# The P V products of a pair of heads in one run of eight matmuls instead of two runs of four

## The reference

```
# block 1: 16 heads of 32, softmax over all 512 keys
q, k, v = split(xn @ W_qkv)                       # xn: normalised, scaled and shifted x
logits = einsum('bhqd,bhkd->bhqk', rms(q), rms(k)) * 32 ** -0.5
o = einsum('bhqk,bhkd->bhqd', softmax(logits), v)
y = o + o @ W_out
# block 2: 16 heads of 32, rotary parts, causal mask
scores = where(causal, einsum('bqhd,bkhd->bhqk', q, k) * 32 ** -0.5, min)
out = einsum('bhqk,bkhd->bqhd', softmax(scores), v) @ o_w
# then h + shared expert + 2 of 7 routed experts, chosen by a router
```

## Time and profile before

| | |
|---|---|
| median of 3 runs | 1286.12 us (1280.24 to 1286.89) |
| the profiled execution | 1280.03 us, of which the span 1278.3 us |
| attention stream | about 74 to 950 us of the span |
| experts | about 950 us to the end |
| granted clock of TensorE, mean | 0.955 |

### The profile page before, as it was taken

The page is one execution under the profiler, slowest core; times in us unless marked ns, Lnnn a source line. Parts: engine busy times, 40 slices in busy tenths (PEclk is TensorE's granted clock), DMA queues, the critical chain, the costliest instruction groups (busy, mean ns, idle before and its releaser), DMA issues.

```text
span 1278.3 us, 18202 instructions
## 1 busy us (share of the span) xinstructions
PE 1146.9 (90%) x5687; PEld 803.5 (63%) x5687; DVE 729.0 (57%) x1714; ACT 571.8 (45%) x1248; POOL 331.9 (26%) x275
## 2 busy tenths in 40 slices
PE   5989999999999799999979979988889999999970
PEld 5745555665566356557657657755657888888860
DVE  6565685477545756656545675475445774444433
ACT  3324464455444455555455554454454753222220
POOL 1313133201310131002012201200134464555530
PEclk9979999999999899999989999998979999999995
DMA  7054344235323732464476365385456745656669
GB/s 257 34 182 117 94 142 140 61 118 189 112 63 98 229 111 65 157 175 117 155 201 193 114 221 153 97 255 171 114 199 227 253 140 107 111 107 114 113 127 345
DMA packets 107470, 191.11 MB, mean 150 GB/s; under 512 B 26000, under 2 KB 36656, under 8 KB 105840
## 3 DMA queue, kind: packets, MB, share of 16 engines
q1 hardware_dynamic: 98560, 169.62, 42.6%
q0 software_dynamic: 8512, 19.93, 8.7%
q10 hardware_dynamic: 304, 0.40, 0.1%
HBM read 118.98 MB, written 65.53 MB: 144 GB/s over the span
## 4 chain that ended last, share of the span: by engine, by line
PE 73%; DVE 8%; DMA 7%; issue 4%; ACT 4%; SPq 3%; POOL 0%; DVEq 0%; ACTq 0%; POOLq 0%
PE psum L930 12%; PE psum L747 9%; PE psum L748 8%; PE psum L749 8%; PE psum L893 6%; PE psum L914 6%; PE psum L1008 4%; PE psum L1010 4%; PE psum L1009 4%; PE psum L756 3%; PE psum L1035 2%; PE psum L977 2%; PE psum L1037 2%; PE psum L1036 2%; DMA inverse_s<-prob_sums 1%
## 5 line engine op out<-in xcount | busy, mean ns | idle before, releaser
L1252 ACT ACTIVATE probs<-psum 128x512 f32<-128x512 f32 (+3 forms) x512 | 255.9, 517 | 224.9 <-PE psum L917 112.1
L1676 DVE TENSOR_REDUCE nmax<-psum 128x1 f32<-128x512 f32 x256 | 171.0, 685 | 112.7 <-PE psum L893 108.0
L893 PE MATMUL psum<-stack 96*128 96x512 f32 (+3 forms) x512 | 211.3, 418 | 17.9 <-DVE nmax L1679 11.0
L914 PE MATMUL psum<-stack 97*128 97x512 f32 (+3 forms) x512 | 202.3, 396 | 22.9 <-ACT probs L1252 20.5
L930 PE MATMUL psum<-probs,vals 128*33 128x512 f32 (+3 forms) x1024 | 212.2, 537 | 0.0
L893 PEld LDWEIGHTS psum<-stack 96*128 96x128 f32 x512 | 101.9, 199 | 80.7 <-issue 56.8
L1679 DVE CUSTOM_DVE_ANT_0 psum<-psum,causal 128x128 f32<-128x128 f32 (+3 forms) x256 | 122.7, 503 | 32.7 <-PE psum L893 31.5
L914 PEld LDWEIGHTS psum<-stack 97*128 97x128 f32 x512 | 101.7, 199 | 51.0 <-ACT probs L1252 27.2
L930 PEld LDWEIGHTS psum<-probs,vals 128*33 128x33 f32 x1024 | 50.3, 113 | 101.7 <-issue 69.5
L747 PE MATMUL psum<-w_hi,xh 128*128 128x512 f32 (+1 forms) x256 | 95.4, 373 | 3.2 <-DVEq L1532 1.6
L748 PE MATMUL psum<-w_hi,xl 128*128 128x512 f32 (+1 forms) x256 | 93.6, 366 | 0.0
(11 more groups left out here) (245 smaller groups left out, 2291.5 us busy)
## 6 DMA issues: line engine op xcount, KB each, us to landing
stack<-split_s SPq DMA_DIRECT2D x378, 128.0 KB, 3.2
split_s<-split SPq DMA_DIRECT2D x64, 512.0 KB, 3.0
inverse_sums<-inverse_s SPq DMA_DIRECT2D x124, 64.0 KB, 2.4
xt<-in_x_dram SPq DMA_DIRECT2D x4, 1024.0 KB, 5.4
x_s<-yt SPq DMA_DIRECT2D x4, 1024.0 KB, 5.5
xt<-x_s SPq DMA_DIRECT2D x4, 1024.0 KB, 5.0
yt<-in_x_dram SPq DMA_DIRECT2D x4, 1024.0 KB, 5.6
res<-x_s SPq DMA_DIRECT2D x4, 1024.0 KB, 8.4
```

The source lines that it names most:

```text
L893: sq.filled(nc.tensor.matmul(psum[:, sq.bank(M), 0:n], st[:, 0, t * P:(t + 1) * P], st[:, 1, 0:n], start=True, stop=True), M)
L914: last = nc.tensor.matmul(psum[:, bank, lo:S], st[:, 1, t * P:(t + 1) * P], st[:, 0, lo:S], start=True, stop=not masked)
L1252: sk.cleared(nc.scalar.activation(probs[:, M % NX, lo:S], psum[:, sk.bank(M), lo:S], ACT.Exp, scale=SCALE), M)
L1676: sq.cleared(V.tensor_reduce(out, psum[:, sq.bank(M), :], AX.X, ALU.max, negate=True), M)
```

## The change

Two constants are changed; the buffers of exponentials stay eight.

```
-GROUP = 4
-NX = 2 * GROUP
+GROUP = 8
+NX = 8
```

## The result

The change makes the kernel slower. Before 1285.38 us (1280.24 to 1286.89), after 1305.44 us (1303.82 to 1307.73), ratio 1.0184 with a 95% interval of 1.0155 to 1.0213. The forecast was 1282, the range 1270 to 1295: wrong in sign and outside the range.

What follows compares the result with a forecast made beforehand. TensorE, busy for 90% of the span, was taken to bound 35 of 64 pairs; -11.9 - 0.6 + 2.4 + 2.2 + 2.0 + 0 + 1.7 = -4.2 us, from 1286.12 to 1281.9 us; range 1270 to 1295.

Steps and rivals of the forecast that it cites:

- kind 1: 35 pairs in which TensorE is full: one run fewer saves 0.34 us in each, -11.9 us in all.
- the saving isn't a run's: Rival: the 0.34 us belongs to the change of data, not to entering a run; 1293.8 us, chance 0.05.
- Kind 6: The other 13 pairs: a chain beginning before the run sets their end, eight pv beside it as before; 0 us.
- Kind 2: Six light pairs paced by ACT, among pairs 5 and 6 of batches 0 to 3: gain eaten, -0.1 each, -0.6 us.
- Kind 3: Pairs 7 of batches 0 to 3, with transposes of x: waits for exponentials queued on ACT, +0.6 each, +2.4 us.
- kind 5: Pairs 4 and 5 of batch 0, full of DVE work: late copy and lost shelter, +1 each, +2.0 us.
- Kind 4: Four pairs where the maxima's DMA, taken to land in 1.8 us, delays the next pair's scores_t: +2.2 us.
- second rival: Late maxima after an unbroken half pair, at scores_t of step 8 in light pairs; 1294.4 us, chance 0.2.
- kind 7: One more fall of TensorE's clock, at places where it already has gaps: +1.7 us, from 0 to +7.
- Both still lie inside the run: Pairs 4 to 7: ACT's keys copy at step 0, 1.3 us late, and one DVE operation end within the run of eight.
- the prediction's example: A run of four at the lower clock, 3.59 us instead of 1.91, after scores_t had waited 1.9 us.

Runs made afterwards that it cites:

- by2: Kernel before with runs of two pv in place of four in all pairs, the same eight buffers; 1298.53 us, ratio 1.0139.
- packed2: Changed kernel with block 2's exponentials packed so that those of tile 0 wait for no product; 1307.75 us, ratio 1.0197.
- nine: Changed kernel with nine buffers of exponentials in place of eight in batches 0 to 2; 1307.33 us, ratio 1.02.
- wait: Kernel before, runs of four kept, with the exponentials of steps 0 and 1 waiting for pv as in the changed kernel; 1305.45 us, ratio 1.0168.
- fives: Kernel before with a run of eight only in pair 5 of batches 1 to 7; 1295.7 us, ratio 1.0095.

## Why the prediction was wrong, step by step

- **A run costs 0.34 us (kind 1): right as a price, too much as a gain.** A run of eight and its distance to the next product, the answer to the earlier trace rows:

```profile
227.77 0.40 PE L914 MATMUL psum<-stack 97*128 97x512 f32 x1
228.10 3.63 PE L930 MATMUL psum<-probs,vals 128*33 128x512 f32 x16
231.66 0.50 PE L893 MATMUL psum<-stack 96*128 96x512 f32 x1
```

  3.56 us to the next product, as forecast. 32 of the 35 pairs gained 9.4 us; without pair 2 of batch 0 and its shifted 1.8, 31 gained 7.5, 0.24 each and not 0.34: 0.35 in pairs 0 to 2 of batches 1 and 2, 0.02 to 0.13 in their other full pairs, 0.23 in batches 4 to 6. Their products are shorter there, which I hadn't priced apart; why the gain is smaller wasn't traced. The sorting failed in three (pair 3 of batches 0 and 1, pair 2 of batch 7), +6.7. The rival that the saving isn't a run's falls, by `by2` as well (0.33 a run).
- **Kind 6, "so 0": the step that failed.** I argued that the chain which sets these pairs' ends begins before the run, so that eight pv stand beside it before as after. In pair 5 of batch 6 that isn't so. Before, then after, from the half pair on:

```profile
834.62 1.70 PE L930 MATMUL psum<-probs,vals 128*33 128x512 f32 x8
...
840.02 0.30 PE L893 MATMUL psum<-stack 96*128 96x128 f32 x1 [2.63 <-DVE nmax L1679]
...
841.46 1.23 PE L930 MATMUL psum<-probs,vals 128*33 128x256 f32 x8
```

```profile
855.19 0.44 PE L893 MATMUL psum<-stack 96*128 96x128 f32 x1 [2.64 <-DVE nmax L1679]
...
857.81 3.33 PE L930 MATMUL psum<-probs,vals 128*33 128x512 f32 x16
```

  DVE's chain for that `scores` (a copy of transposed queries, the norms, the division, maxima) runs without a pause from the copy of step 2 on, before and after:

```profile
833.85 0.69 DVE L1517 TENSOR_TENSOR split<-psum,split 128x512 fp32r<-128x512 f32 x1 [1.11 <-ACT split L1094]
```

```profile
849.05 0.69 DVE L1517 TENSOR_TENSOR split<-psum,split 128x512 fp32r<-128x512 f32 x1 [1.12 <-ACT split L1094]
```

  That is over 2 us behind the end of the run of step 1 (831.66 and 846.61), not before its start, and `scores` follows 6.2 and 6.1 us later. The run of 1.7 us lay inside these 6 and cost nothing; after, the wait is still 2.64 us, and the pv come behind it, partly at the lower clock (3.33 us). `packed2` shows that the chain hangs on the run's end. There ACT doesn't wait for the buffer, and DVE's copy of step 0 stands 1.8 us before the end of the run of eight (848.62, the end 850.38) instead of at it (846.59, 846.61). Yet copy and `scores` keep their distance to the run's end (both line numbers are 16 higher in that kernel):

```profile
852.54 0.69 DVE L1533 TENSOR_TENSOR split<-psum,split 128x512 fp32r<-128x512 f32 x1 [1.25 <-ACT split L1110]
...
858.68 0.45 PE L909 MATMUL psum<-stack 96*128 96x128 f32 x1 [2.64 <-DVE nmax L1695]
```

  From the run's end to that `scores` it is 8.4 us before, 8.6 after and 8.3 in `packed2`: what sets the pair's end begins with the first products behind the run. Forecast 0 for 13 pairs, measured +14.8 (13.1 without the shift in pair 1 of batch 0), of which the pairs 5 of batches 5 to 7 hold 8.7. I had read such a chain in one pair only, pair 1 of batch 7, and that one came out 0.9 shorter.
- **Kind 2: right for pair 6, wrong for pair 5.** I walked through one pair, pair 6 of batch 3, and took it for six. It came out at 9.71 (forecast 9.5). In its neighbour, DVE, not ACT, sets the pace once the run is gone: +1.2 instead of -0.1, and +3.2, with a fall of the clock, in pair 5 of batch 2. DVE's 6.47 us of work in 9.70 had looked harmless, but 4.3 of them are one piece. The Trainium skill ("Perfetto Trace Analysis", Matmul Optimizations) wants matmuls back to back in batches, because the engine scales its power with its utilization. Larger batches went with less time in the full pairs (16.25 to 15.89 us) and with more in this one (9.70 to 10.89), at a granted clock of 1.00 in all four stretches, so neither difference bears on the page's reason.
- **Kind 3: mis-sized; kind 5: right in one pair of two.** Kind 3 took +5.8 against +2.4, of which pair 7 of batch 1 alone +2.4 with a fall of the clock (its clock is 1.00 in `nine`, and there it loses 0.87). The waits for exponentials did grow in pairs 7 of batches 0 to 2, by 0.5, 0.5 and 0.8 us; in batch 3 the new wait is another, 1.3 us of the transposes for DVE's copy of x. In kind 5, pair 5 of batch 0 lost 1.0 us, as forecast; pair 4 gained 2.9, because a wait of 2.3 us and a fall that stood in it are gone from it while pair 3 lost 4.5.
- **Kind 4, the maxima: near by luck.** +3.0 against +2.2, but `scores_t` waits for the maxima 2.2 us in three places, against 1.8 in two before. The only new wait of the four pairs, 1.0 us, is in pair 0 of batch 7, where the clock fell as well (+2.6); pair 5 of batch 4 lost 1.9 without any wait for maxima, and pair 6 of batch 2 got 1.8 shorter. In pair 6 of batch 3 the DMA left at 555.81 and its rows were used at 557.74, so it landed within 1.9 us, where I had taken 1.8. The second rival gave 1294.4, nearest to the result, but the runs with the maxima a step earlier rule late maxima out as the cause.
- **The clock (kind 7): mis-sized.** I took one more fall, +1.7. By the mean clocks, 141 us against 115 lie at the lower level, 26 more; the mean is within the 0.01 that I had allowed, so that test was too coarse. 26 us at half speed cost up to 13 if TensorE worked throughout. Pair 3 of batch 0 after shows one, the answer to the earlier trace rows:

```profile
149.76 0.67 PE L893 MATMUL psum<-stack 96*128 96x512 f32 x1 [1.47 <-DVE nmax L1676]
...
152.01 5.93 PE L930 MATMUL psum<-probs,vals 128*33 128x512 f32 x16
```

  After a wait of 1.47 us the products last 0.67 instead of 0.40 us, and the run of eight takes 5.93 instead of 3.63, 2.3 more; a run of four so caught took 1.7 more.
- **"Both still lie inside the run": right.** `nine` and `packed2` bear it out for batches 0 to 2 and block 2, the trace of pair 5 for batch 3.

What stays open: how much of the loss in the other 32 pairs is the clock's share, up to about half; why two pv after step 7 save half of it; whether the buffer's wait matters in batch 3; and why `wait` loses as much in batches 5 to 7 as it does, where falls of the clock cover the reading.

## To carry to other kernels

Work on the critical engine that stands in the middle of a stretch paced by others is hidden there, and moving it to the stretch's end makes it bare, even if it saves its own overhead; where the engine is full, the same move gains. So sort the places first and choose the grouping for each: one length for all lost 1.8% here, three lengths won 1.3%. And for a chain said to begin before a point, look up its first instruction on the slower engine, and its longest unbroken piece of work, not its share of busy time.

## What the runs showed of the hardware

One cause has two prices: the missing cover in pair 5 of batch 3 costs 1.2 us in the changed kernel, at a granted clock of 1.00, and 4.2 us in `fives`, at 0.75, with the same instructions in the pair. Entering and leaving a run of pv costs 0.33 to 0.36 us in pair 1 of batch 1, with runs of two, four and eight. A wait of 1.47 us stood ahead of a fall, shorter than the 1.9 us of the prediction's example. And the 76 products of zeros raised the mean granted clock from 0.946 to 0.967 and left the time where it was.
